# A transformer block on one core: attention multiplied in place in its PSUM banks, and the float32 stages of TensorE in three runs a batch

## The reference

```python
x = x + attn(layernorm(x), Wq, bq, Wk, bk, Wv, bv, Wo, bo)
x = x + ffn(layernorm(x), gamma, beta, fc1_q, ..., fc2_bias)
# attn, in chunks of 128 tokens, for each of 16 heads of width 16:
q = elu(h @ Wq.T + bq) + 1;  k = elu(h @ Wk.T + bk) + 1;  v = h @ Wv.T + bv
scores = where(tril, q @ k.T, 0)
num = scores @ v + q @ S                    # S: sum of k.T @ v over earlier chunks
den = sum(q * (cumsum(k) + z))              # z: sum of k over earlier chunks
out = (num / den) @ Wo.T + bo
# ffn: h2 = layernorm(x) * gamma + beta; w = (q - 128) * scales
y = silu(h2 @ w1 + fc1_bias);  x + 0.5 * (y @ w2 + fc2_bias)
```

## Time and profile before

| | us |
|---|---|
| median of 3 runs | 1485.08 |
| lowest, highest | 1481.96, 1494.12 |
| profiled execution | 1479.71, its span 1478.0 |
| TensorE, share of the span busy | 95% |
| VectorE, ScalarE, GpSimd | 78%, 74%, 46% |
| mean granted TensorE clock | 0.984 |

### The profile page before, as it was taken

The page is one execution under the profiler, slowest core; times in us unless marked ns, Lnnn a source line. Parts: engine busy times, 40 slices in busy tenths (PEclk is TensorE's granted clock), DMA queues, the critical chain, the costliest instruction groups (busy, mean ns, idle before and its releaser), DMA issues.

```text
span 1478.0 us, 61027 instructions
## 1 busy us (share of the span) xinstructions
PE 1402.7 (95%) x25746; PEld 1234.7 (84%) x25746; DVE 1155.6 (78%) x2014; ACT 1087.9 (74%) x1789; POOL 674.9 (46%) x473
## 2 busy tenths in 40 slices
PE   7669999999999999999999999999999999999978
PEld 6558888888888888888888888888888888888867
DVE  5478788778878777878877878877787887787755
ACT  4267787777778777778777778877777877777753
POOL 2133554444455443455444355544445544435543
PEclk8789999999999999999999999999999999999999
DMA  5112012222111222201222211122211122221010
GB/s 150 46 44 58 16 43 55 57 57 57 34 29 50 57 57 57 56 14 44 57 57 57 57 19 43 52 57 57 57 43 24 47 57 57 57 57 19 27 45 29
DMA packets 93538, 72.09 MB, mean 49 GB/s; under 512 B 8768, under 2 KB 92992, under 8 KB 93504
## 3 DMA queue, kind: packets, MB, share of 16 engines
q1 hardware_dynamic: 92144, 71.59, 19.3%
q10 hardware_dynamic: 1360, 0.01, 0.1%
HBM read 38.03 MB, written 16.78 MB: 37 GB/s over the span
## 4 chain that ended last, share of the span: by engine, by line
PE 49%; issue 19%; DVE 15%; POOL 10%; ACT 6%; DVEq 1%; POOLq 0%; DMA 0%; ACTq 0%
PE sc L292 26%; POOL s_lo L986 9%; DVE res L683 5%; PE sc L416 3%; DVE gt_lo L705 3%; PE num L358 3%; DVE stats L563 3%; PE ring L429 2%; PE num L359 2%; ACT silu_f L830 2%; DVE silu_f L626 2%; ACT s_hi L845 1%; ACT silu_f L838 1%; PE num L474 1%; PE sc L331 1%
## 5 line engine op out<-in xcount | busy, mean ns | idle before, releaser
L986 POOL TENSOR_TENSOR s_lo<-silu_f,s_hi 128x512 fp32r<-128x512 f32 x256 | 351.1, 1387 | 472.8 <-ACT s_hi L845 471.4
L292 PE MATMUL sc<-w_hi,s_hi 128*128 128x256 f32 x992 | 285.9, 288 | 20.6 <-POOL s_lo L986 20.5
L292 PE MATMUL sc<-w_lo,s_hi 128*128 128x256 f32 x992 | 280.5, 283 | 0.0
L292 PE MATMUL sc<-w_hi,s_lo 128*128 128x256 f32 x992 | 280.3, 283 | 0.0
L292 PEld LDWEIGHTS sc<-w_hi,s_hi 128*128 128x128 f32 x992 | 189.8, 191 | 31.6 <-DVE phi_q L597 24.7
L838 ACT ACTIVATE silu_f<-silu_f 128x512 f32<-128x512 f32 x256 | 159.1, 622 | 58.0 <-DVE silu_f L626 57.8
L292 PEld LDWEIGHTS sc<-w_lo,s_hi 128*128 128x128 f32 x992 | 190.0, 192 | 0.0
L292 PEld LDWEIGHTS sc<-w_hi,s_lo 128*128 128x128 f32 x992 | 189.9, 191 | 0.0
L636 DVE TENSOR_TENSOR probs<-sc,causal 128x1024 f32<-128x1024 f32 x128 | 153.4, 1220 | 29.2 <-PE sc L416 29.2
L845 ACT ACTIVATE s_hi<-silu_f 128x512 fp32r<-128x512 f32 x256 | 160.9, 628 | 5.2
L626 DVE SCALAR_TENSOR_TENSOR silu_f<-sc,scale,silu_f 128x512 f32<-128x512 f32 x127 | 95.0, 748 | 88.8 <-ACT silu_f L830 86.7
(11 more groups left out here) (195 smaller groups left out, 3908.8 us busy)
## 6 DMA issues: line engine op xcount, KB each, us to landing
x_in<-in_x SPq DMA_DIRECT2D x32, 512.0 KB, 4.5
rb<-den_rows SPq DMA_DIRECT2D x256, 64.0 KB
xb<-in_x SPq DMA_DIRECT2D x32, 512.0 KB, 5.1
out<-out_t SPq DMA_DIRECT2D x64, 256.0 KB, 4.2
probs<-in_q SPq DMA_DIRECT2D x2, 512.0 KB, 8.3
silu_f<-in_q SPq DMA_DIRECT2D x2, 512.0 KB, 6.3
res<-in_sc SPq DMA_DIRECT2D x1, 512.0 KB, 7.0
out_t<-in_sc SPq DMA_DIRECT2D x1, 512.0 KB, 9.1
```

The costliest lines, as they stand in the source:

```text
L292: last = e.matmul(target, a, b, start=(n == 0), stop=(n == 3 * len(pairs) - 1))
L986: sl.done(e.tensor_tensor(s_lo[:, j, :], silu_f[:, j % SLOTS, :], s_hi[:, j, :].bitcast(F32), ALU.subtract))
```

## The change

Five things are changed together.

1. attention() is one multiplication over both halves and is written back into the banks of num; rb is only read. attention_hi and attention_lo are one pass each and read the banks, so num is freed by at_l.
2. The residual and its bias are made in two halves, with an event for each.
3. TensorE's order: x_transposes go behind from_states, chunk_states, scores(1) and values(0) stand together, values(1), from_states and x_transposes stand together, and denominators go to the end, ahead of the next batch's ffn_in.
4. VectorE's, ScalarE's and GpSimd's orders follow. x_hat of batch i+1 is computed in the middle of iteration i and not at the end of iteration i-1; reciprocals are last; input_bias is ahead of ffn_lo(0); the norm's power comes last on GpSimd.
5. The bank table is new. SyncE's order of transfers is as it was, only the broadcasts wait for attention instead of attention_lo.

```diff
         BANKS = {
+            "ht0": (1,), "ht1": (7,), "kt0": (6,), "kt1": (0,), "sc0": (2, 3, 4, 5), "f0a": (6,), "f0b": (1,), "f1a": (0,),
+            "f1b": (7,), "kv": (6,), "sc1": (2, 3, 4, 5), "num": (0, 1), "f2a": (6,), "f2b": (3,), "f3a": (2,),
+            "f3b": (7,), "f4a": (6,), "f4b": (5,), "xt0": (2,), "xt1": (6,), "f5a": (4,), "f5b": (3,), "f6a": (7,),
+            "f6b": (5,), "f7a": (2,), "f7b": (6,), "k0": (7,), "q0": (3,), "k1": (5,), "q1": (2,), "v0": (4,), "v1": (6,),
+            "wo0": (0,), "wo1": (1,), "z0": (0,), "z1": (4,), "den": (3,),
         }
...
-            "xt0": (xt_l, 0), "xt1": (xt_l, 1), "kv": (summed, 0), "num": (attn, 1),
+            "xt0": (xt_l, 0), "xt1": (xt_l, 1), "kv": (summed, 0), "num": (at_l, 0),
...
             scores(0)
             fc1(0)
-            x_transposes(0)
-            x_transposes(1)
             fc1(1)
             chunk_states()
-            fc1(2)
             scores(1)
             values(0)
+            fc1(2)
             fc1(3)
             fc1(4)
             values(1)
-            fc1(5)
             from_states(0)
             from_states(1)
+            x_transposes(0)
+            x_transposes(1)
+            fc1(5)
             fc1(6)
             fc1(7)
...
             fc2(0)
             fc2(1)
-            denominators()
             fc2(2)
             fc2(3)
+            denominators()
...
-            def attention(t):
+            def attention():
...
-                by_chunk = rb[:, t, :].rearrange("p (m r q) -> p r m q", r=2, q=HALF)
-                attn.done(e.tensor_tensor(
-                    by_chunk, num[:, :, t * 2 * P:(t + 1) * 2 * P].rearrange("p r (m q) -> p r m q", q=HALF),
-                    by_chunk, ALU.mult))
+                attn.done(e.tensor_tensor(num_view, num_view, by_half(rb[:, :, :]), ALU.mult))
...
-            def residual():
+            def residual(h, shift=-1):
...
-                for c in range(C):
+                for c in range(2 * h, 2 * h + 2):
...
-            def attention_lo(t):
+            def attention_lo():
...
-                at_l.done(e.tensor_tensor(gt_lo[:, t, :], rb[:, t, :], gt_hi[:, t, :].bitcast(F32), ALU.subtract))
+                at_l.done(e.tensor_tensor(by_half(gt_lo[:, :, :]), num_view, by_half(gt_hi[:, :, :].bitcast(F32)),
+                                          ALU.subtract))
...
             ffn_sum(0)
+            sum_states()
+            mask(1, 0)
+            ffn_sum(1)
+            mask(1, 1)
+            ffn_sum(2)
+            ffn_sum(3)
+            if N:
+                ve_x_hat(e, w, 1)
+            residual(0)
+            ffn_sum(4)
             input_lo(0)
             input_lo(1)
...
             ffn_sum(5)
-            residual()
+            attention()
             ffn_sum(6)
...
             ffn_sum(7)
...
+            residual(1)
+            attention_lo()
+            add_residual(0)
+            features(0)
+            add_residual(1)
+            norm_x1()
+            features(1)
+            features(2)
+            cumulate(0)
+            features(3)
+            cumulate(1)
+            norm_factors()
...
+            final(0)
             if N2:
                 ve_norm_x(e, w, 2)
...
             if N:
                 final(1)
+            reciprocals()
...
             ffn_scaled(0)
+            ffn_scaled(1)
+            ffn_silu(0)
+            ffn_hi(0)
+            ffn_scaled(2)
+            ffn_silu(1)
+            ffn_scaled(3)
+            ffn_scaled(4)
+            ffn_hi(1)
+            ffn_silu(2)
+            ffn_hi(2)
+            ffn_silu(3)
             input_hi(0)
             input_hi(1)
...
+            ffn_scaled(5)
+            ffn_scaled(6)
             ffn_hi(3)
...
             ffn_silu(4)
             ffn_hi(4)
             ffn_silu(5)
...
+            ffn_silu(6)
+            ffn_scaled(7)
             ffn_hi(5)
...
+            attention_hi()
+            ffn_silu(7)
             ffn_hi(6)
...
+            ffn_hi(7)
             table_exp()
...
             ffn_norm()
+            table_silu()
...
+            input_bias()
             ffn_lo(0)
-            input_bias()
             ffn_lo(1)
             ffn_lo(2)
             ffn_lo(3)
+            residual_bias(0)
             ffn_lo(4)
             ffn_lo(5)
-            residual_bias()
             ffn_lo(6)
+            ffn_lo(7)
+            ln2_factors()
+            query_sums(0)
+            residual_bias(1)
+            query_sums(1)
             if N2:
                 po_norm(e, w, 2)
...
             def sp_reciprocals():
 
+                w.need(attn, 0)
                 w.need(rden, 1)
-                w.need(at_l, 0)
```

More of the change, by code:

```diff
@@ L352, in fc1 @@
                         w.need(e_x1, -1)
-                        w.need(attn, -1)
+                        w.need(at_l, -1)
                         w.need(e_out, -2, 0)
@@ L669, in final @@
                 w.need(z_pe, shift, n)
-                w.need(e_res, shift)
+                w.need(e_res[n], shift)
                 w.need(store, shift - 1)
@@ L675, in final @@
                     in1=res[:, cs, :].rearrange("p c d -> p (c d)"), op0=ALU.mult, op1=ALU.add))
-            def residual():
-                if not Fn:
+            def residual(h, shift=-1):
+                if not (A if shift == 0 else Fn):
                     return
-                w.need(res_c, -1)
-                w.need(e_out, -2)
-                for c in range(C):
+                w.need(res_c, shift)
+                w.need(e_out, shift - 1, h)
+                for c in range(2 * h, 2 * h + 2):
                     last = e.tensor_scalar(res[:, c, :], x1[:, c, :], res_mul[:, c:c + 1], res_add[:, c:c + 1],
                                            ALU.mult, ALU.add)
-                res_m.done(last)
+                res_m[h].done(last)
             def ffn_input_lo(t):
@@ L711, in add_residual @@
                 w.need(e_hn2, -1)
+                w.need(res_m[n], -1)
                 w.need(wo_pe, 0, n)
@@ L775, in ve_iteration @@
             ffn_sum(0)
+            sum_states()
[6 more added lines that the diff above has]
+                ve_x_hat(e, w, 1)
+            residual(0)
+            ffn_sum(4)
             input_lo(0)
             input_lo(1)
[L778 to L784, removed]
             ffn_sum(5)
-            residual()
+            attention()
             ffn_sum(6)
-            attention(0)
-            attention(1)
             ffn_sum(7)
@@ L792, in ve_iteration @@
                 preparation[3]()
-            attention_lo(0)
-            attention_lo(1)
+            residual(1)
+            attention_lo()
[9 more added lines that the diff above has]
+            norm_factors()
+            if preparation[1]:
+                preparation[1](0)
+                preparation[1](1)
+            final(0)
             if N2:
                 ve_norm_x(e, w, 2)
[L797 to L814, removed]
             if N:
                 final(1)
+            reciprocals()
         def ac_iteration(e, i, A, Fn, N, N2, preparation=None):
@@ L909, in input_hi, with attention_hi @@
                 xt_h.done(e.activation(xt_hi[:, t, :], use_bank(f"xt{t}"), ACT.Copy))
-            def attention_hi(t):
+            def attention_hi():
                 if not A:
                     return
-                w.need(attn, 0, t)
+                w.need(attn, 0)
                 w.need(f_pe, -1)
-                at_h.done(e.activation(gt_hi[:, t, :], rb[:, t, :], ACT.Copy))
+                at_h.done(e.activation(by_half(gt_hi[:, :, :]), num_view, ACT.Copy))
             def table_exp():
@@ L992, in input_bias, with residual_bias @@
                 e_xb.done(e.tensor_tensor(xb[:, :, :], xb[:, :, :], bias_o[:, None, :].to_broadcast([P, C, D]), ALU.add))
-            def residual_bias():
-                if not Fn:
+            def residual_bias(h, shift=-1):
+                if not (A if shift == 0 else Fn):
                     return
-                w.need(res_m, -1)
-                e_res.done(e.tensor_tensor(res[:, :, :], res[:, :, :], bias_2[:, None, :].to_broadcast([P, C, D]), ALU.add))
+                w.need(res_m[h], shift)
+                cs = slice(2 * h, 2 * h + 2)
+                e_res[h].done(e.tensor_tensor(res[:, cs, :], res[:, cs, :], bias_2[:, None, :].to_broadcast([P, 2, D]), ALU.add))
             def query_sums(t):
@@ L1179, in _ @@
             count(e.tensor_tensor(causal[:, :], causal[:, :], causal_2[:, :], ALU.add))
-            early(e, e_res, sl)
+            early(e, *e_res, sl)
             po_norm(e, Waiter(e, -1), 1)
@@ L1202, in _ @@
             e.memset(state_keep[:, :], 1.0).then_inc(p_par, 1)
-            early(e, ht_l, f_b, e_out, res_m)
+            early(e, ht_l, f_b, e_out, *res_m)
             e.wait_ge(p_const, 12)
```

44 lines of the change are left out of this document (11 added, 33 removed), and 5 rows, old and new, of the table BANKS.

## The result

The changed kernel takes 1761.4 us (median of 4, 1760.9 to 1762.5) against 1485.6 of the kernel before (median of 4): 1.185 times as long, 95% interval 1.180 to 1.190. The profiled execution's span is 1759.1 us.

A forecast was written before the change was run, and what follows sets the result against it. TensorE's own work was taken as the bound, 44.06 us a batch; less 1.79 gained, plus 9.1 and 1.45 of waits and 1.2 for the clock, 54.0. Over all batches 300 more than before: 1783 us, range 1705 to 1850.

The forecast's parts named there:

- The chain: Late xb delays GpSimd's bias and s_lo(0), then ScalarE's ffn_scaled(4), then TensorE in x_transposes(1): 9.94 us a batch more.
- The stall with what follows it: TensorE waits 9.1 us in x_transposes(1), then 1.45 for xt_lo, plus 1.2 for the clock, each batch.
- The gain: TensorE's batch shortens by 0.74 us from float32 runs and 1.05 from the s_lo stall: 1.79 saved.
- issue to the start of the bias: From xb's issue on SP to GpSimd's start: 5.89 us in the trace, taken as 5.5.
- fc1(7) waiting for xt_lo: On TensorE, fc1(7) takes the bank of xt0 and waits 1.1 us, and 0.35 more for xt_lo(1).
- an allowance of 1.1: Half clock for 5.5 us costs 2.7, less 1.1 in which fc1(6) would wait anyway: 1.6; 1.2 taken.
- The term for a run: TensorE's float32 stages go from seven runs a batch to three: leaving one costs 0.11 us, entering about 0.1.
- The term of 1.05 for s_lo(7): GpSimd's s_lo(7) goes ahead of the norm power, so fc2(0) on TensorE no longer waits: 1.05 us a batch.
- stall and gain cancel: Rival (b): xb lands near 12.5, or GpSimd reaches the bias only then; 1485 us within 1%, chance 0.03.
- the copy isn't waited for: Rival (a): the late copy xb holds nothing up and the gain stands; 1430 us, chance 0.07.
- The fast landing: Rival (c): xb lands 2.3 to 3 us earlier, no clock loss beyond the slack; 1690 to 1715 us, chance 0.06.
- the clock stays low longer: Rival (d): TensorE at half pace through the projections, 4.9 us instead of 1.2; 1890 us, chance 0.07.

The follow-up runs named there:

- bias in sixth place: Changed kernel with only GpSimd's input_bias moved from ahead of ffn_lo(0) to behind ffn_lo(5): 1487.0 us, ratio 1.0019 to the kernel before.
- asking for it first: Changed kernel with only SyncE's order changed, copy xb asked for ahead of the load of x: 1700.8 us, ratio 1.146 to the kernel before.
- x_hat earlier: Changed kernel with input_bias behind ffn_lo(5) and x_hat ahead of ffn_sum(3) on VectorE: 1462.9 us, ratio 0.988; a second time 1465.1 us.
- the clock kept up: Changed kernel with 34 unread products of 512 columns on TensorE between x_transposes(0) and (1): 1752.2 us, ratio 1.180 to the kernel before.
- alone in the old kernel: Kernel before with one edit, the norm's power on GpSimd behind ffn_lo(7) and not ahead of it: 1478.5 us, ratio 0.997.
- the two with the reciprocals at their old place: Changed kernel, denominators and reciprocals moved back: with xb asked for first, bias first, 1634.9 us; with bias sixth, x_hat ahead of ffn_sum(3), 1636.3 us.

## Why the prediction held, and where it did not

**The chain.** It held link by link. The profile shows the wait for xb on GpSimd (17.8 us a batch in the mean, 15 to 19 foretold), ScalarE's stop at ffn_scaled(4) (10.7, about 12 foretold), TensorE's in x_transposes(1) for ScalarE (7.8 in the mean, about 9 foretold), the dip of the clock in each batch, and no wait of fc2(0). The runs show the cause: one instruction of GpSimd's order decides over 274 us (bias in sixth place), the copy is late from x_hat and from the reciprocals both (asking for it first left 5.4 of 7.8 us in the mean), and once it is early TensorE doesn't stop there even with the bias in front.

**The size.** 9.24 us a batch were lost and 9.94 foretold; with the outer batches 276 us against 298. Part of that nearness is luck. The stall with what follows it was put at 11.75 us (9.1, 1.45 and 1.2); beside the kernel that lacks it, the one with x_hat earlier, it is 53.18 - 43.03 = 10.15. The gain was put at 1.79 and is 0.91. So the loss was taken 1.60 too large and the gain 0.88 too large, and the two errors work against each other.

| term | foretold | measured |
|---|---|---|
| xb asked for | t = 14.3 | 15.5 |
| issue to the start of the bias | 5.5 | 4.73 |
| ffn_scaled(4) starts | t = 23.5 | 23.9 |
| TensorE's wait in x_transposes(1) | 9.1 | 8.16 |
| fc1(7) waiting for xt_lo | 1.45 | none at low clock, 1.09 with the clock kept up |
| clock | 1.2 | 0.56, by keeping it up |

xb was later because the walk left out that scores(0) now wait for the reciprocal (0.49), which shifts the masks, and a short wait of VectorE for TensorE (0.33) before x_hat; the other one there, 0.44 for ScalarE, it had. It landed faster. No stores ran beside it this time (DMA share 0.06 from 743 to 744, against 0.53 to 0.71 from 709 to 711 in the kernel before), but that this is the reason is not shown; the 5.89 us from which the prediction started was also one of the slowest of that kernel (4.9 to 6.0 in ten batches, 5.2 in the median). The later issue and the faster landing nearly cancel. TensorE came 1.1 later to the place of its stall, by the same scores and by values(0), so it waited less there. The last two terms are one: I had taken them as a sum with an allowance of 1.1, and the allowance was too small. Together they made 2.65; from the last x transposition to the first projection the kernel after takes 5.48 us (753.41 to 758.89) and the one with the bias sixth 3.19 (724.58 to 727.77), so they are 2.29.

Three slips in the prediction's own numbers are of no weight: its terms add up to 1785 and not 1783, its range ends 5 us below its own upper bound of 1855, and what it first says of fc1(7) it later says of fc1(6).

**The gain.** This was the weak part of the sum. I had 1.79 us a batch coming from three float32 runs and the absent wait for s_lo. With both new stalls away the kernel is 0.91 a batch faster than the one before, not 1.79. The term for a run was about right, 0.2 for leaving and entering one against 0.1 to 0.25 measured.

The term of 1.05 for s_lo(7) was read from a wait without asking what ends next behind it: alone in the old kernel it is worth 0.10, for the sake of the bank of q0. In the new bank table z0 takes the bank of wo0, and there the traces show the term whole. This is the last matmul of output_projection in the kernel before, which fc2(0) follows at 736.75, 1.17 later:

```profile
735.58 0.28 PE L292 MATMUL sc<-wo_hi,gt_lo 128*128 128x256 f32 x1
```

And the same place in the kernel with x_hat earlier, where fc2(0) follows after 0.12:

```profile
728.54 0.28 PE L298 MATMUL num<-wo_hi,gt_lo 128*128 128x256 f32 x1
728.66 0.28 PE L298 MATMUL num<-w_hi,s_hi 128*128 128x256 f32 x1
```

What the sum lacked are two costs. scores(0) now wait for the reciprocal, because sc0 takes banks 2 to 5 and den has bank 3: k_transposes(1) is over at 709.32 in the kernel with the bias sixth and scores start at 709.98, 0.66 later, where it was 0.09 in the kernel before (707.07, 707.16), so 0.57. And values(0) spans 1.78 us in the mean of eight batches with x_hat earlier, where it had spanned 1.48. 1.79 - 0.57 - 0.30 = 0.92, against the 0.91 measured. This is worked out from rows; no run takes the two away with nothing else changed.

Had nothing been said of the late copy, my forecast would have been 1430, for a kernel that in truth, without its stall, stands at 1487.

**The rivals.** That stall and gain cancel, or that the copy isn't waited for, fell with the trace. The fast landing was half right: 3.9 to 4.7 us from issue to bias when the copy goes alone (nine batches of the run that asks for it first, 4.2 in the median), and 4.3 to 4.7 behind the load. The estimate from the Trainium skill ("DMA: Bandwidth & Descriptors", Anatomy of one DMA) was 3.2; that section fits transfers issued from GpSimd, and these are issued by SyncE. That the clock stays low longer did not come: 4.8 to 6 us.

**Open.** values(0) spans 1.58 to 1.91 us in every kernel here whose reciprocals come last, and 1.48 or 1.49 in the kernel before and in the two with the reciprocals at their old place. The order chunk_states, scores(1), values(0) is the same in those two, so it is not the cause by itself. In the slow ones SyncE's eight broadcasts are still being issued while it runs (731.23 to 738.58 in the kernel after, with values(0) from 736.57 on); in the others they are over. No wait is recorded inside it, and whether the broadcasts are the cause is not shown. The attention in place, its single passes and the residual in halves were not run by themselves either: that they cost nothing rests on the sum above alone.

## What to carry to other kernels

When an instruction moves to the front of an in-order queue, look up when its input arrives in the new order, not in the old one: the producer's producer may have moved too, and here two such moves and a third in the queue of the reader met. A stall is worth its length only if no other wait ends just behind it; before it goes into a sum as a gain, ask what the same instruction needs besides (here a bank, which one bank table frees in time and the other does not). And a version that is slower by one wait is worth mending before it is given up: moving two instructions took this one from 1761 to 1463 us.

## What the runs showed of the hardware

Small VectorE instructions can take as long as GpSimd's beside them. In the kernel after, a multiplication of 128 by 4 elements starts while GpSimd adds the residual's bias (777.17 to 779.39):

```profile
777.17 2.22 POOL L1001 TENSOR_TENSOR res<-res,bias 128x512 f32<-128x512 f32 x1
779.35 1.30 POOL L1008 TENSOR_TENSOR qk<-qk,phi_q 128x512 f32<-128x512 f32 x1
```

```profile
778.23 1.19 DVE L741 SCALAR_TENSOR_TENSOR hn_add<-mv,ln_rstd 128x4 f32<-128x4 f32 x1
...
779.40 1.26 DVE L744 SCALAR_TENSOR_TENSOR res_add<-mv,ln_rstd 128x4 f32<-128x4 f32 x1
```

It takes 1.19 us, and 0.15 in the kernel before, where GpSimd is idle at that point. The two VectorE instructions end at 779.42 and 780.66, the two of GpSimd at 779.39 and 780.65. By the Trainium skill ("SBUF — State Buffer", Who interferes with whom) a VectorE instruction with two inputs in SBUF contends with a GpSimd instruction that reads SBUF, for ports that only one of them holds at a time. These rows agree: each of the two VectorE instructions ends when GpSimd's does.

attention_lo, which reads one operand from the banks and one from SBUF, takes 1.21 us for 1024 columns beside GpSimd at work; before, the two halves, with both operands in SBUF, took 2.35. GpSimd was at work beside the first of them only (729.02 to 730.31), so why they took so long is not shown.

From the start of the issue of a 512 KB copy to the start of the bias it took 3.9 to 4.7 us when the copy was alone on the queue, 4.3 to 4.7 behind another of the same size, and 4.9 to 6.0 with two stores just ahead as well.
